# A convolution stage on one core: the first unit's second-half points and sums on GpSimd, its first half's on VectorE, and the second unit's first-point copy and middle outputs at the head of their windows

## The reference

```
x = x + L0(group_norm(x))      # channel layer norm, 1x1 and depthwise 3x3 convolutions, 8-head channel attention, 1x1 projection
x = x + L1(group_norm(x))      # 1x1, 3x3, 5x5 and dilated 3x3 convolutions, concatenated, then a 1x1 convolution
```

## Time and profile before

| | |
|---|---|
| median of 3 runs | 1710.65 us (1710.39 to 1711.21) |
| the profiled execution, its own time | 1710.78 us |
| its span in the trace | 1709.1 us |
| TensorE matmuls busy | 1653.3 us (97%) |
| VectorE busy | 1490.5 us (87%) |
| ScalarE busy | 1015.0 us (59%) |
| GpSimd busy | 580.1 us (34%) |
| TensorE's mean granted clock | 0.975 |

### The profile page before, as it was taken

One profiled execution on the slowest core, in us unless ns is written; L12 is line 12 of the kernel. 1 busy time (PEld: TensorE's weight loads), 2 busy tenths in 40 slices (PEclk: granted clock), 3 DMA queues, 4 the chain that ended last, 5 costly groups with the idle time before them and its releaser, 6 DMA issues.

```text
span 1709.1 us, 38211 instructions
## 1 busy us (share of the span) xinstructions
PE 1653.3 (97%) x13285; PEld 1552.4 (91%) x13285; DVE 1490.5 (87%) x1962; ACT 1015.0 (59%) x1651; POOL 580.1 (34%) x398
## 2 busy tenths in 40 slices
PE   6999999999999999999999999999999999999998
PEld 5989969999999996999999996899999999599998
DVE  6788879999888858999978886999998887799997
ACT  2866677455285658644546666755446566765551
POOL 5799941222282003232247002123316400312222
PEclk9999979999999997999999999899999999799999
DMA  8012115666501201566630220356661121055553
GB/s 192 0 41 61 47 32 129 169 166 171 151 18 56 74 19 39 149 171 176 164 105 15 69 65 1 87 160 173 166 170 46 33 74 42 1 134 138 134 145 104
DMA packets 105017, 166.01 MB, mean 97 GB/s; under 512 B 40266, under 2 KB 78763, under 8 KB 104780
## 3 DMA queue, kind: packets, MB, share of 16 engines
q1 hardware_dynamic: 81772, 138.95, 32.0%
q10 hardware_dynamic: 23168, 26.04, 4.7%
HBM read 52.20 MB, written 25.17 MB: 45 GB/s over the span
## 4 chain that ended last, share of the span: by engine, by line
PE 84%; DVE 7%; issue 4%; ACT 3%; DMA 1%; DVEq 0%; SPq 0%; ACTq 0%
PE ps L948 42%; PE ps L787 12%; PE ps L808 8%; PE ps L810 7%; PE ps L809 7%; PE ps L836 3%; PE ps L870 3%; PE ps L943 1%; PE ps L750 1%; ACT region L1150 1%; ACT region L1083 1%; DVE region L1665 1%; DVE X L1473 1%; DVE region L1632 0%; ACT region L1131 0%
## 5 line engine op out<-in xcount | busy, mean ns | idle before, releaser
L948 PE MATMUL ps<-region,W 128*96 128x256 f16 (+2 forms) x7140 | 800.6, 270 | 9.4 <-ACT region L1207 4.5
L948 PEld LDWEIGHTS ps<-region,W 128*96 128x96 f16 (+1 forms) x7140 | 771.4, 122 | 31.1 <-issue 13.8
L1387 DVE TENSOR_TENSOR region<-V,band 128x2322 f32<-128x2322 f32 (+2 forms) x104 | 256.8, 2479 | 60.3 <-PE ps L810 57.2
L1150 ACT ACTIVATE region<-region 96x1584 f16<-96x1584 f32 (+2 forms) x80 | 98.4, 1272 | 309.2 <-DVE region L1569 309.2
L695 POOL TENSOR_TENSOR region<-region 96x528 f32<-96x528 f32 (+1 forms) x72 | 91.8, 1279 | 446.1 <-DVE region L1635 328.6
L808 PE MATMUL ps<-region 128*128 (+1 forms) x1152 | 228.1, 280 | 10.0 <-DVE region L1396 4.4
L810 PE MATMUL ps<-region 128*128 (+1 forms) x1152 | 222.7, 275 | 0.0
L809 PE MATMUL ps<-region 128*128 (+1 forms) x1152 | 222.2, 274 | 0.0
L1665 DVE SCALAR_TENSOR_TENSOR region<-ps,small,region 96x768 f32<-96x768 f32 (+1 forms) x220 | 203.8, 988 | 12.1 <-PE ps L948 10.4
L787 PE MATMUL ps<-proj,region 96*128 96x240 f32 x1024 | 208.9, 367 | 0.0
L787 PEld LDWEIGHTS ps<-proj,region 96*128 96x128 f32 x1024 | 194.8, 191 | 13.1
(11 more groups left out here) (220 smaller groups left out, 2193.8 us busy)
## 6 DMA issues: line engine op xcount, KB each, us to landing
region<-region SPq DMA_DIRECT2D x104, 247.5 KB, 3.9
region<-in_x_dram SPq DMA_DIRECT2D x128, 192.0 KB, 2.4
out_dram<-region SPq DMA_DIRECT2D x40, 576.0 KB, 4.2
region<-region ACTq DMA_DIRECT2D x72, 247.5 KB, 2.4
X<-in_x_dram SPq DMA_DIRECT2D x30, 576.0 KB, 6.2
region<-region SPq DMA_DIRECT2D x32, 247.4 KB, 4.9
X<-in_x_dram SPq DMA_DIRECT2D x19, 384.0 KB, 12.1
region<-region SPq DMA_DIRECT2D x24, 185.6 KB, 3.6
```

The lines of the kernel that those rows point to most:

```text
L948: last = mm(o, w, src, start=k == 0, stop=k == len(steps) - 1, skip_group_check=split and ck > 0)
L1150: act.activation(dst[0:C, a:e, x:z], src, ACT.Copy, scale=1.0 if whole else col(SA)).then_inc(s_h, 1)
L1387: v.tensor_tensor(T[:, i, 3 * c:3 * c + m].rearrange("p m (i j) -> p m i j", j=3), taps.broadcast_to([P, m, BW // 3, 3]), mask.broadcast_t ...
```

## The change

Four things are moved. (1) GpSimd's `first_planes` no longer makes planes 3 and 4 out of the differences nor the sum of plane 3; it makes planes 0, 1, 2 of blocks 1 to 4 and their sums instead. (2) VectorE makes planes 3 and 4 of all blocks in `first_part` and both first-half sums in one step; of the second half it makes only the edge block's pieces. (3) ScalarE's mean step (`one`) stands behind the square root, and waits for VectorE's planes. (4) In the window of the second unit (m = 1) ScalarE does the first-point copy before `hi` of unit 2, and VectorE the middle outputs of unit 0 before the planes of unit 2; this window is taken out of the loops, which are shifted by one window.

```
@@ gpsimd: first_planes
-                    done(3)
-                    take(twice, plane(1, 5, 4), plane(1, 5, 3))
-                    done(5)
-                    take(plane(1, 5, 3), twice, plane(1, 5, 3))
-                    for n in (8, 10):
-                        for c in range(2):
-                            take(slots(4, 5, c)[:, :, 0], slots(4, 5, c)[:, :, 0], taps(1, c, 1)[:, :, 0])
-                        done(n)
-                    pool.tensor_tensor(cs[0][:, 1:5, 0:PC], plane(1, 5, 3)[:, :, PC:RW], plane(1, 5, 3)[:, :, 1:1 + PC],
-                                       ALU.add).then_inc(s_fp, 1)
                     for c in range(2):
                         take(slots(0, 3, c), taps(2, c, 3), taps(0, c, 3))
+                    done(6)
+                    take(twice, plane(1, 5, 1), plane(1, 5, 0))
+                    take(plane(1, 5, 2), plane(1, 5, 2), plane(1, 5, 1))
+                    done(8)
+                    take(plane(1, 5, 0), twice, plane(1, 5, 0))
+                    take(plane(1, 5, 2), plane(1, 5, 2), plane(1, 5, 1))
+                    done(10)
+                    pairs = pln[:, 1:5, 0:3 * RW].rearrange("p k (q e) -> p k q e", e=RW)
+                    pool.tensor_tensor(cs[1][:, 1:5].rearrange("p k (q j) -> p k q j", j=PC), pairs[:, :, :, PC:RW],
+                                       pairs[:, :, :, 1:1 + PC], ALU.add).then_inc(s_fp, 1)
@@ scalar
-                act.wait_ge(s_fp, b * NFP + 10 + START)
-                act.wait_ge(s_st, sv + N_MEAN2 + 2 + START)
+                deviation(N_PPRE + b * NPST + 7, 7, 1)
+                act.wait_ge(s_pl0, b * NPL0 + 5 + START)
                 act.activation(one, one, ACT.Identity, bias=col(MG2)).then_inc(s_fix, 1)
-                deviation(N_PPRE + b * NPST + 7, 7, 1)
...
                     def midway():
-                        if whole > 1:
+                        if whole > 1 and not point_first:
                             first_point(m, i, BPU)
...
                     act.wait_ge(s_cv, n * NCV + START)
+                    if point_first:
+                        first_point(m, i, BPU)
...
-                with act.Fori(0, PAIRS - 1) as k2:
+                window(1, 1, 0, 2, 2, point_first=True)
+                with act.Fori(1, PAIRS) as k2:
+                    window(k2 * 2, 0, k2, 2, 2)
                     window(k2 * 2 + 1, 1, k2, 2, 2)
-                    window(k2 * 2 + 2, 0, k2 + 1, 2, 2)
-                window(UNITS - 4, 1, PAIRS - 1, 2, 2)
@@ vector: first_part, first_sums, second_part_edge, second_part
-                    v.scalar_tensor_tensor(plane0(0, 3, 4), plane0(0, 3, 4), -2.0, plane0(0, 4, 5),
-                                           ALU.mult, ALU.add).then_inc(s_pl0, 1)
+                    v.scalar_tensor_tensor(slot(3), slot(3), -2.0, slot(4), ALU.mult, ALU.add).then_inc(s_pl0, 1)
+                    first_done(3)
+                    for c in range(2):
+                        one = pln0[:, 1:5, 4 * RW + c * PC + 1:4 * RW + c * PC + 1 + HC]
+                        v.scalar_tensor_tensor(one, rows[:, 0, c], -2.0, one, ALU.mult, ALU.add).then_inc(s_pl0, 1)
...
-                    v.tensor_tensor(cs0[0][:, 0, 0:PC], plane0(0, 3, 4)[:, PC:RW], plane0(0, 3, 4)[:, 1:1 + PC],
-                                    ALU.add).then_inc(s_pl0, 1)
                     dve.wait_ge(s_fix, b + 1 + START)
-                    one = pln0[:, :, 4 * RW:5 * RW]
-                    v.tensor_tensor(cs0[0][:, :, PC:2 * PC], one[:, :, PC:RW], one[:, :, 1:1 + PC], ALU.add).then_inc(s_pl0, 1)
+                    pairs = pln0[:, :, 3 * RW:PLAIN].rearrange("p k (q e) -> p k q e", e=RW)
+                    v.tensor_tensor(cs0[0].rearrange("p k (q j) -> p k q j", j=PC), pairs[:, :, :, PC:RW],
+                                    pairs[:, :, :, 1:1 + PC], ALU.add).then_inc(s_pl0, 1)
...
-                    slot = lambda k: pln0[:, :, k * RW:(k + 1) * RW]
-                    first_done(6)
-                    dve.wait_ge(s_fp, b * NFP + 13 + START)
+                    slot = lambda k: plane0(0, k, k + 1)
+                    first_done(7)
                     v.scalar_tensor_tensor(slot(0), slot(0), -2.0, slot(1), ALU.mult, ALU.add).then_inc(s_pl0, 1)
                     v.scalar_tensor_tensor(slot(2), slot(1), -2.0, slot(2), ALU.mult, ALU.add).then_inc(s_pl0, 1)
@@ vector: window
+                    if outputs_first:
+                        middle_outputs(m - 1, BPU)
                     planes(m + 1, whole)
-                    middle_outputs(m - 1, BPU)
+                    if not outputs_first:
+                        middle_outputs(m - 1, BPU)
```

More of the change, by code:

```diff
@@ L326, in build_program @@
         NPL, NH, NL, NCV, NACC = 8, 8, 4, 5, 11
-        NFP, NPL0 = 13, 9
+        NFP, NPL0 = 11, 10
         later = lambda b, u: b * (UNITS - 1) + u
@@ L1210, in first_point, with window @@
                                    ACT.Copy, scale=col(OSC_MHALF)).then_inc(s_t1, 1)
-                def window(m, i, k2, whole, ahead):
+                def window(m, i, k2, whole, ahead, point_first=False):
                     n = b * UNITS + m
                     def midway():
-                        if whole > 1:
+                        if whole > 1 and not point_first:
                             first_point(m, i, BPU)
@@ L1495, in first_part @@
                     first_done(2)
-                    v.scalar_tensor_tensor(plane0(0, 3, 4), plane0(0, 3, 4), -2.0, plane0(0, 4, 5),
-                                           ALU.mult, ALU.add).then_inc(s_pl0, 1)
+                    dve.wait_ge(s_fp, b * NFP + 3 + START)
+                    slot = lambda k: pln0[:, :, k * RW:(k + 1) * RW]
+                    v.scalar_tensor_tensor(slot(3), slot(3), -2.0, slot(4), ALU.mult, ALU.add).then_inc(s_pl0, 1)
+                    first_done(3)
+                    rows = X[:, 2 * W:(2 + 4 * OR) * W].rearrange("p (k r j c) -> p r c k j", r=OR, j=HC, c=2)
@@ L1518, in second_part @@
                     v.scalar_tensor_tensor(slot(2), slot(1), -2.0, slot(2), ALU.mult, ALU.add).then_inc(s_pl0, 1)
-                    first_done(8)
-                    pairs = pln0[:, :, 0:3 * RW].rearrange("p k (q e) -> p k q e", e=RW)
-                    v.tensor_tensor(cs0[1].rearrange("p k (q j) -> p k q j", j=PC), pairs[:, :, :, PC:RW],
-                                    pairs[:, :, :, 1:1 + PC], ALU.add).then_inc(s_pl0, 1)
+                def second_part():
+                    first_done(9)
+                    pairs = plane0(0, 0, 3).rearrange("p (q e) -> p q e", e=RW)
+                    v.tensor_tensor(cs0[1][:, 0].rearrange("p (q j) -> p q j", j=PC), pairs[:, :, PC:RW],
+                                    pairs[:, :, 1:1 + PC], ALU.add).then_inc(s_pl0, 1)
@@ L1708, in outer_outputs, with window @@
                     outputs(u, blocks, slice(0, 3, 2))
-                def window(m, i, k2, whole):
+                def window(m, i, k2, whole, outputs_first=False):
+                    if outputs_first:
+                        middle_outputs(m - 1, BPU)
                     planes(m + 1, whole)
-                    middle_outputs(m - 1, BPU)
+                    if not outputs_first:
+                        middle_outputs(m - 1, BPU)
                     lows(m + 1, 1 - i, k2 + i, whole)
@@ L1729, in _ @@
                 first_rows(0, 0, BPU)
-                with dve.Fori(0, (UNITS - 3) // 2) as k2:
+                window(1, 1, 0, 2, outputs_first=True)
+                with dve.Fori(1, (UNITS - 3) // 2) as k2:
+                    window(k2 * 2, 0, k2, 2)
                     window(k2 * 2 + 1, 1, k2, 2)
-                    window(k2 * 2 + 2, 0, k2 + 1, 2)
+                window(UNITS - 3, 0, (UNITS - 3) // 2, 2)
                 window(UNITS - 2, 1, (UNITS - 3) // 2, UNITS - 1)
```

11 lines of the change are left out of this document (5 added, 6 removed).

## The result

The changed kernel took **1714.9 us** (median of 11 runs, 1713.94 to 1716.41) and the kernel before, run beside it, 1710.37 us (11 runs, 1709.48 to 1711.44): the ratio is 1.0026, with a 95% interval of 1.0018 to 1.0033. So it is slower by 4.5 us. The profiled execution took 1714.65 us, with a span of 1712.9 us.

A forecast was written before the change was run, and what follows sets the result against it. VectorE was taken to bound the kernel, with TensorE following it through the copy. Image losses of 0.65 + 0.55 + 0.85 + 0.75 = 2.8 us on 1710.78 us gave 1713.6 us, range 1709.0 to 1716.0 us.

The forecast's parts named there:

- within 0.2%: Whole kernel: a time within about 0.2% (3.4 us) of no change, chance 0.54, against 0.36 for slower.
- The first part: First unit, image 1: VectorE's longer first part makes the first `hi` 1.28 us later and the low parts 1.63 us later.
- The second part: First unit's second half: low parts at the same time, a gain of 1.27 us and a loss of 1.28 us cancelling.
- GpSimd's cover: First unit: GpSimd's 15.4 us of work hidden by VectorE's L1473; uncovered, a step would cost 1.3 to 2 us.
- The held VectorE: Second unit's window: `hi` of unit 2 waits for the copy behind late TensorE; VectorE loses 0.55 to 0.85 us.
- Moving the two middle outputs ... costs nothing in sum: Second unit's window: VectorE's two outputs (0.75 us) ahead of the planes add nothing in sum, planes come 0.73 us later.
- The clock: Rival, chance 0.05: 2.4 us idle before the first matmul lowers TensorE's clock, 2 us lost in each image, 1722 us.
- the first part is hidden: Rival, chance 0.10: VectorE's first steps fit into its square-root wait, 4 x 1.2 us gained, 1706 us.
- the hold doesn't reach VectorE: Rival, chance 0.15: TensorE only some 0.8 us later, copy done before unit 2's planes, 1710.8 us.
- The large stalls: TensorE's four large waits, 4.5 us: removing them is worth nothing; about 1 us returns at group 2 of unit 2.

The follow-up runs named there:

- E4: Kernel before, with GpSimd also making the second half's points and sums of blocks 1 to 4, VectorE only the edge block's: 1719.81 us, ratio 1.0052.
- E3: Kernel before with part 4 of the change alone (copy and middle outputs first in the second unit's window): 1713.15 us, ratio 1.0014.
- E8: Kernel before with only VectorE's half of part 4 (middle outputs first), the copy where it was: 1713.16 us, ratio 1.0016.
- E2: The change without part 4, windows and loops as in the kernel before: 1711.09 us, ratio 1.0001.
- E10: The change with the copy of unit 1 back behind `hi` of unit 2, middle outputs still first: 1714.45 us, ratio 1.0019.
- E5: Kernel before with VectorE's two steps for planes 0 and 2 moved ahead of its first low parts: 1705.06 us, ratio 0.9973.
- E7: The change with 26 filler calls instead of 22: 1715.84 us, ratio 1.0030.
- E1: The change with 30 filler calls instead of 22 ahead of the first unit: 1715.75 us, ratio 1.0027.
- E9: E5 with 30 filler calls instead of 22: 1706.71 us, ratio 0.9978 to the kernel before.
- E11: E5 plus plane 2 of blocks 1 to 4 on GpSimd, with 28 filler calls instead of 22: 1706.26 us, ratio 0.9974 to the kernel before.

## Why the prediction was right or wrong

The direction was right and the time is in the range, 1.3 us above the value given; "within 0.2%" had the larger chance, and it is slower by 0.26%. The range was hit partly by luck: 2.8 us of loss were forecast and 4.5 measured, and a third of these came from a fall of the clock that the forecast left out.

- **The first part**: right. The first `hi` came 1.31 us later (predicted 1.28), the low parts 1.58 (1.63), TensorE's first matmul 1.57. The two strided steps took 0.42 us each, for 0.45. The durations of rows carried this. By the table of the Trainium skill (VectorE: DVE Perf Modes, the section on the TRN2 errata) the three steps would have ended sooner, an estimate that the prediction put at 0.25 us (redone from its own terms it is 0.34), and the trace disagrees with that row.
- **The second part**: right. It came at the same time, 0.06 us earlier, as worked out; the three steps became waiting.
- **GpSimd's cover**: its length was right (15.3 us from 646.97 to 662.24, for 15.4), its price was not. It ends 0.6 us before the mark. "A step of GpSimd's would cost its 1.3 to 2 us" looked for the cost at the tensors that GpSimd hands over; E4 shows that it lies at VectorE's two-input steps beside it, 3.6 us.
- **The held VectorE**: the place was right, a wait of 0.56 us before L1641, and `hi` of unit 2 at 37.61 us (predicted 37.57). For images 1, 2 and 3 the sum of the losses at the low parts was put at 2.15 us and is 1.97; the single terms were less good, 0.55, 0.85 and 0.75 us for 0.69, 0.61 and 0.67. And half of the sum has another cause than the one given: part 4 alone costs 0.33 us in an image (E3). "Moving the two middle outputs ... costs nothing in sum" was the failed step: E8 shows that it costs 0.27 us at the low parts with the copy where it was. The gap that the outputs filled was not counted. By the prediction's own terms (planes that allow `hi` at 698.4, and 1.55 us from `hi` to the low parts) it would have been 0.1 us; from `hi` to the low parts it took 1.66 us. The late TensorE adds the rest, 0.28 to 0.36 us over E3. It is not a sum of terms in which each would be saved by itself: take the copy back and most of the outputs' cost remains.
- **The windows outside the loop**: not in the sum; 0.10 us for each of two, of which 0.10 us is left at the end of an image, so 0.4 us in four.
- **The clock**: named as a rival at 0.05, for all images at 2 us each. It came in one image of the profiled execution, with 1.64 us at the first 24 matmuls (4.47 for 2.83) and 1.5 us at VectorE. This is the largest missed term: image 0 was put at 0.65 us and lost 2.28. The error was to reason with one idle time, 2.4 us, for the four images; they are 1.82 and 2.91 us in images 1 and 0, since the fillers end when the clock lets them. Without that fall the sum would be some 3.1 us, 1713.5 us against the median of 1710.37; the lowest run is 1713.94, and no profile shows the change without a fall.
- **The other rivals**: E2 shows that the first part is hidden from the end, but not as the rival had it: the first `hi` was 1.3 us late, the second half's was not, and nothing was gained. The rival in which the hold doesn't reach VectorE fell by the 0.28 to 0.36 us over E3 and by the pair of E10.
- **The large stalls** behind the copy were worth nothing, as said. There were three of them, not the prediction's four. E3 removes the one at unit 1 and finds it again at unit 2, and the change has it there too, with 0.89 us for the "about 1 us" said.

## What to carry to other kernels

Where one engine is full and another only follows it, a wait of the follower isn't a gain to be had: ask whether the step moved to end it now stands between that follower and the full engine, for then each delay of the follower arrives in full (a fall of the clock cost 1.5 us for 0.46, E2). And the earlier the full engine runs, the less slack is left for such a delay: with VectorE 1.37 us ahead a fall cost 1.3 us (E5). Short steps between a producer's signal and a wait for the answer are cover; count what fills the gap when they leave. And the one useful part of this change was an order of steps, not a choice of engine: moving the two plane steps ahead of the low parts (E5) gave 5.8 us with no work moved to another engine.

## What the runs showed of the hardware that was not expected

- Beside GpSimd's tensor steps, VectorE's steps with two SBUF inputs of one element for each partition took 0.94 to 1.90 us for 0.15 to 0.21; steps with one tensor input kept their time (E4).
- The granted clock fell to 0.50 for 3.4 us behind waits of TensorE of 1.95, 2.22, 2.39 and 2.58 to 2.98 us, and stayed at 1.00 behind others of up to 2.49 us (E8, image 0, before group 2 of unit 1; E2, image 2, 2.31 before its first matmul), so the length of the wait doesn't decide it alone in these traces. The Trainium skill (TensorE: Matmul & The Clock Gate, Part 1) says that idleness halves the clock; the trace agrees. A fall cost 1.3 to 1.7 us at the 24 matmuls that the rows show (4.12 to 4.50 us for 2.83).
- A window written out behind or ahead of a loop took 0.1 us more than the same window inside it (change, E3, E8, E10), in window 1 between its low parts and the next planes. The cause wasn't tried.
- With 28 or 30 filler calls in front of the convolution no fall was profiled under it, with 26 one was (E7). Instead placing DMAs came late in two images of each (E1, E9, E11), the same six images in which an instruction packet fell among them. The medians didn't improve.
